# A message-passing layer on one core: gathered rows added by an identity product, laps in pairs, update steps spaced over two laps

## The reference

```python
msg_in = concatenate([nodes[row], nodes[col], edge_features], axis=-1)      # 160 wide
messages = relu(msg_in @ mW1 + mb1) @ mW2 + mb2                             # 128 hidden, 64 out
aggregated = segment_sum(messages, col, num_segments=12500)
upd = relu(concatenate([nodes, aggregated]) @ uW1 + ub1) @ uW2 + ub2
x = layernorm(x + upd)
```

## Time and profile before

| | us |
|---|---|
| median of three runs | 2077.49 |
| lowest and highest of them | 2075.89, 2080.76 |
| the profiled execution | 2080.34 |
| its span, first to last instruction | 2078.6 |

### The profile page before, as it was taken

One profiled execution on the slowest core, in us unless ns is written; L12 is line 12 of the kernel. 1 busy time (PEld: TensorE's weight loads), 2 busy tenths in 40 slices (PEclk: granted clock), 3 DMA queues, 4 the chain that ended last, 5 costly groups with the idle time before them and its releaser, 6 DMA issues. The chain is left out here.

```text
span 2078.6 us, 61063 instructions
## 1 busy us (share of the span) xinstructions
PE 1452.0 (70%) x10272; PEld 1305.0 (63%) x10272; DVE 1428.5 (69%) x7986; ACT 1202.2 (58%) x7120; POOL 1407.3 (68%) x1480
## 2 busy tenths in 40 slices
PE   6866677667666776676667767767767767677765
PEld 5766666566666666666666666666656666566664
DVE  3677677677776777777776667676666676666765
ACT  3366566566565655665656556556556566556563
POOL 1677777777777777777777666666666666666661
PEclk8898888787888888888887778777777777778777
DMA  9833332333333333333322222222222222222221
GB/s 217 231 86 83 82 84 81 80 86 81 82 81 83 85 81 81 85 82 82 79 76 76 69 67 66 69 70 73 66 68 65 70 72 69 68 64 66 72 70 28
DMA packets 179217, 170.23 MB, mean 82 GB/s; under 512 B 78164, under 2 KB 142090, under 8 KB 178842
## 3 DMA queue, kind: packets, MB, share of 16 engines
q0 software_dynamic: 46944, 96.24, 17.8%
q1 hardware_dynamic: 118298, 64.35, 11.4%
q10 hardware_dynamic: 13698, 7.28, 1.7%
HBM read 151.34 MB, written 16.36 MB: 81 GB/s over the span
## 5 line engine op out<-in xcount | busy, mean ns | idle before, releaser
L312 POOL DMA_INDIRECT ag<-src_table,slot_idx x1467 | 1400.7, 955 | 629.4 <-issue 420.2
L290 DVE COPY own_x<-xc 64x4 uint8 x6144 | 682.9, 193 | 131.8 <-issue 124.1
L300 ACT ACTIVATE own_x<-xc 64x4 uint8 x6144 | 634.1, 190 | 183.2 <-issue 182.3
L350 PE MATMUL bank<-picked,picks 128*128 128x128 f32 x3128 | 586.5, 342 | 62.5 <-ACT picks L382 40.0
L350 PEld LDWEIGHTS bank<-picked,picks 128*128 128x128 f32 x3128 | 508.4, 244 | 91.4 <-issue 56.8
L367 PE MATMUL bank<-oh,hid 128*128 128x96 f32 x3128 | 518.2, 321 | 49.8 <-ACT hid L392 49.6
L367 PEld LDWEIGHTS bank<-oh,hid 128*128 128x128 f32 x3128 | 488.2, 238 | 68.6 <-ACT hid L392 59.1
L414 DVE TENSOR_TENSOR hid<-bank,ag 128x512 f32<-128x512 f32 (+1 forms) x391 | 257.4, 658 | 297.2 <-issue 161.1
L382 ACT ACTIVATE picks<-bank 96x512 f32<-96x512 f32 x391 | 230.6, 590 | 225.7 <-PE bank L336 127.3
L392 ACT ACTIVATE hid<-hid 128x512 f32<-128x512 f32 x343 | 215.1, 627 | 241.4 <-DVE hid L414 238.9
L336 PE MATMUL bank<-ident_bf,oh 128*96 128x128 bf16 x1564 | 192.2, 258 | 227.4 <-DVE oh L400 227.2
(11 more groups left out here) (63 smaller groups left out, 446.2 us busy)
## 6 DMA issues: line engine op xcount, KB each, us to landing
picks<-edge_t SPq DMA_DIRECT2D x391, 64.0 KB
ag<-src_table,slot_idx POOLq DMA_INDIRECT x1467
picked<-dst_table SPq DMA_DIRECT2D x391, 48.0 KB
src_table<-ag SPq DMA_DIRECT2D x25, 256.0 KB, 4.1
dst_table<-picks SPq DMA_DIRECT2D x17, 256.0 KB, 4.5
xc<-x_t ACTq DMA_DIRECT2D x8, 400.0 KB, 15.6
resid<-x_rows SPq DMA_DIRECT2D x24, 128.0 KB
out<-resid ACTq DMA_DIRECT2D x24, 128.0 KB
```

The source lines that it names most:

```text
L290: done = copy(own_x[:, c:c + 1].bitcast(u8), xc[0:D, :].bitcast(u8)[:, ds(offset, 4)])
L300: return nc.scalar.activation(to, of, ACT.Copy)
L312: pool.indirect_dma_start(out=ag[:, k, j * DH:(j + 1) * DH], out_offset=None, in_=src_table, in_offset=bass.IndirectOffsetOnAxis(ap=slot_i ...
L350: last = nc.tensor.matmul(ps_h[q][:, j * DH:(j + 1) * DH], picks[:, r, j * P:(j + 1) * P], picked[:, r, :], start=True, stop=j < own)
```

## The change

- `ag[:, k]` is no longer added by VectorE. `hidden` starts with one product of the identity (float32) with the 512 gathered columns (256 for the own group) into `ps_h`, then the own products, then the four products as before, all accumulating. TensorE waits for the gather; `s_pre` is gone, and a gather waits for `s_h` of the group eight before. `relu` reads `ps_h` and writes `hid`.
- VectorE copies 20 own columns a group, ScalarE 12. `own_x` and its list have two buffers: the copies of one whole lap serve the product of the next, which is at k = 4 now. The list comes in one DMA a lap.
- `slot_idx` has two buffers; one DMA a lap, at k=2, brings the next lap's indices.
- Laps are written in pairs in each loop, since the buffers alternate by lap.
- The update of a chunk is spread over two laps, with m1, m2, m3 at k = 3, 5, 7.
- ScalarE does one square root at the very start, ahead of its first copy.

The diff, cut to its core:

```diff
-OWN_K = 5
+OWN_K = 4
...
-OWN_DVE = 16
+OWN_DVE = 20
-OWN_LATE = (UNROLL - OWN_K) * OWN_N
...
-        slot_idx = sb("slot_idx", [P, UNROLL * TPG], i32)
+        slot_idx = sb("slot_idx", [P, 2, UNROLL * TPG], i32)
...
-        own_late = sb("own_late", [1, OWN_LATE], i32)
-        own_early = sb("own_early", [1, OWN - OWN_LATE], i32)
-        own_x = sb("own_x", [D, OWN])
+        own_list = sb("own_list", [1, 2, OWN], i32)
+        own_x = sb("own_x", [D, 2, OWN])
...
+        def fetch_own_list(sp, lap, par):
+
+            sp.dma_start(own_list[0:1, par, :], own_dram[ds(lap + 1, 1), :]).then_inc(s_own_list, 16)
+
+        def load_own(sp, k, lap, par):
+
+            if k == OWN_K + 1 and not (isinstance(lap, int) and lap == ITERS - 1):
                 if not (isinstance(lap, int) and lap == 0):
-                    sp.wait_ge(s_own_dve, (lap - 1) * UNROLL + UNROLL - OWN_K)
-                    sp.wait_ge(s_own_act, (lap - 1) * UNROLL + UNROLL - OWN_K)
-                sp.dma_start(own_late[:, :], own_dram[ds(lap + 1, 1), 0:OWN_LATE]).then_inc(s_own_late, 16)
+                    sp.wait_ge(s_own_dve, lap * UNROLL)
+                    sp.wait_ge(s_own_act, lap * UNROLL)
+                fetch_own_list(sp, lap + 1, 1 - par)
...
+            if k == 0:
+                eng.wait_ge(s_own_list, (lap + 1) * 16)
...
+            if isinstance(lap, int) and lap == ITERS - 1:
+                return
+            at = k * OWN_N
...
-                c = step * OWN_N + a + n
-                done = copy(own_x[:, c:c + 1].bitcast(u8), xc[0:D, :].bitcast(u8)[:, ds(offset, 4)])
+                c = at + a + n
+                done = copy(own_x[:, 1 - par, c:c + 1].bitcast(u8), xc[0:D, :].bitcast(u8)[:, ds(offset, 4)])
...
+        def gather(pool, g, k, lap, par, tiles=TPG):
+
+
+            if k == 0 and not (isinstance(lap, int) and lap == 0):
+                pool.wait_ge(s_idx, lap * 16)
+            wait(pool, s_h, g - UNROLL + 1)
             pool.sem_inc(s_opened, 1)
...
+                    in_offset=bass.IndirectOffsetOnAxis(ap=slot_idx[:, par, c:c + 1], axis=0),
                 ).then_inc(s_gathered[k], 16)
...
+        def hidden(pe, g, k, lap, par):
 
...
-            wait(pe, s_pre, g - 1)
-            own = TPG - OWN_TILES if has_own(k, lap) else TPG
+            wait(pe, s_relu, g - 1)
+            missing = G_END * TPG - T_END if isinstance(g, int) and g == G_END - 1 else 0
+            wait(pe, s_gathered[k], gathered_of(k, lap) - 16 * missing)
+            w = OWN_AT if has_own(k, lap) else TPG * DH
+            nc.tensor.matmul(ps_h[q][:, 0:w], ident[:, :], ag[:, k, 0:w], start=True, stop=False)
+            if has_own(k, lap):
+                pe.wait_ge(s_own_dve, lap * UNROLL)
+                pe.wait_ge(s_own_act, lap * UNROLL)
+                for j in range(OWN_TILES):
+                    at = OWN_AT + j * DH
+                    nc.tensor.matmul(ps_h[q][:, at:at + DH], own_x[:, par, j * P:(j + 1) * P],
+                                     w_src[0:D, :], start=False, stop=False)
             for j in range(TPG):
                 last = nc.tensor.matmul(ps_h[q][:, j * DH:(j + 1) * DH], picks[:, r, j * P:(j + 1) * P],
-                                        picked[:, r, :], start=True, stop=j < own)
-                if j >= own:
-                    if j == own:
-                        pe.wait_ge(s_own_dve, lap * UNROLL)
-                        pe.wait_ge(s_own_act, lap * UNROLL)
-                    last = nc.tensor.matmul(ps_h[q][:, j * DH:(j + 1) * DH],
-                                            own_x[:, (j - own) * P:(j - own + 1) * P],
-                                            w_src[0:D, :], start=False, stop=True)
+                                        picked[:, r, :], start=False, stop=(j == TPG - 1))
             last.then_inc(s_h, 1)
...
+        def relu(g, k):
             act = nc.scalar
             q = k % 2
-            wait(act, s_pre, g + 1)
-            if has_own(k, lap):
-                act.activation(hid[:, q, OWN_AT:], ps_h[q][:, OWN_AT:], ACT.Relu)
-                act.activation(hid[:, q, 0:OWN_AT], hid[:, q, 0:OWN_AT], ACT.Relu).then_inc(s_relu, 1)
-                return
-            act.activation(hid[:, q, :], hid[:, q, :], ACT.Relu).then_inc(s_relu, 1)
+            wait(act, s_h, g + 1)
+            wait(act, s_agg, g - 1)
+            act.activation(hid[:, q, :], ps_h[q][:, :], ACT.Relu).then_inc(s_relu, 1)
...
-        def add_source(g, k, lap):
...
-            dve.tensor_tensor(hid[:, q, 0:w], ps_h[q][:, 0:w], ag[:, k, 0:w], ALU.add).then_inc(s_pre, 1)
...
+        def next_indices(sp, k, lap, par):
+
+            if k != 2 or isinstance(lap, int) and lap == ITERS - 1:
...
-            half, ahead = (0, 1) if k == UNROLL - 1 else (1, 0)
-            for slot in range(half * HALF, (half + 1) * HALF):
-                sp.wait_ge(s_gathered[slot], gathered_of(slot, lap + ahead - 1))
...
+            wait(sp, s_h, lap * UNROLL)
+            w = UNROLL * TPG
+            sp.dma_start(slot_idx[:, 1 - par, :], src_all[:, ds((lap + 1) * w, w)]).then_inc(s_idx, 16)
...
+        def laps(eng, lap, open_update, finish, chunk):
+
+
+            lap(0, 0, None)
+            lap(1, 1, None)
+            with eng.Fori(1, UPD_LAP // 2) as i:
+                lap(i * 2, 0, None)
+                lap(i * 2 + 1, 1, None)
             open_update()
             behind = eng.value_load(path[0:1, 1:2], min_val=0, max_val=NODES)
             with eng.If(behind < 1):
-                with eng.Fori(UPD_LAP, ITERS - 1) as i:
-                    lap(i, i - UPD_LAP)
-                lap(ITERS - 1, CHUNKS - TAIL - 1)
+                for i in range(UPD_LAP, UPD_LAP + 2):
+                    lap(i, i % 2, i - UPD_LAP)
+                with eng.Fori(UPD_LAP // 2 + 1, (ITERS - 1) // 2) as i:
+                    lap(i * 2, 0, i * 2 - UPD_LAP)
+                    lap(i * 2 + 1, 1, i * 2 + 1 - UPD_LAP)
+                lap(ITERS - 1, 0, CHUNKS - TAIL - 1)
+                finish(CHUNKS - TAIL - 1)
                 chunk([CHUNKS - 2, CHUNKS - 1])
...
+                fetch_own_list(sp, 0, 0)
...
+                        next_indices(sp, k, i, par)
+                        load_own(sp, k, i, par)
...
+            act.wait_ge(s_const, 1)
+            act.activation(stat[:, 0, 0:1], eps[:, :], ACT.Sqrt)
...
-                        if c is not None and k == 6:
-                            act_square(c)
                         own_listed(act, k, i)
                         if exists(g + 1):
                             copy_oh(g + 1, (k + 1) % UNROLL)
-                        if c is not None and k == 6:
-                            act_deviation(c)
                         if exists(g):
-                            relu(g, k, i)
-                        own_columns_act(k, i)
-                        if c is not None and k == 3:
+                            relu(g, k)
+                        own_columns_act(k, i, par)
+                        if before(c) and k == 0:
+                            act_square(c - 1)
+                        elif before(c) and k == 2:
+                            act_deviation(c - 1)
+                        elif before(c) and k == 4:
+                            act_store(c - 1)
+                        elif c is not None and k == 5:
                             act_relu(c)
-                        if c is not None and k == 6:
-                            act_store(c)
-                laps(act, lap, open_update, act_chunks)
+
+                def finish(c):
+                    act_square(c)
+                    act_deviation(c)
+                    act_store(c)
+                laps(act, lap, open_update, finish, act_chunks)
...
-                        if exists(g):
-                            add_source(g, k, i)
...
-                        own_columns_dve(k, i)
-                        if c is not None:
-                            if k == 1:
-                                dve_c2(c)
-                            elif k == 2:
-                                dve_stack(c)
-                            elif k == 5:
-                                dve_center(c)
-                            elif k == 6:
-                                dve_variance(c)
-                                dve_normalize(c)
+                        own_columns_dve(k, i, par)
+                        if before(c) and k == 1:
+                            dve_variance(c - 1)
+                        elif before(c) and k == 3:
+                            dve_normalize(c - 1)
+                        if c is not None and k == 1:
+                            dve_c2(c)
+                        elif c is not None and k == 3:
+                            dve_stack(c)
+                        elif c is not None and k == 7:
+                            dve_center(c)
...
+                def finish(c):
+                    dve_variance(c)
+                    dve_normalize(c)
...
```

(24 more changed lines are left out.)

132 lines of the change are left out of this document (51 added, 81 removed).

## The result

The changed kernel takes 1949.53 us (median of four runs, 1947.02 to 1953.16) against 2077.05 (2075.89 to 2080.76): a ratio of 0.9385, 95% interval 0.9365 to 0.9404. The forecast was 1933, with a range of 1914 to 1990. The profiled execution took 1950.72 us for a span of 1949.0 us; the forecast's sum for that span was 1933.8.

The account below looks back on a forecast made before the run. GpSimd bounds the early laps, and the update laps once TensorE's waits go: span 2078.6 - 133.8 (update laps) - 11 (end) = 1933.8 us, or 1933 us as median; range 1914 to 1990.

Parts of the forecast that it names:

- rival A: The forecast itself: GpSimd is the bound from first gather to last, 1917 to 1958 us; chance 0.64.
- The laps: GpSimd's laps of 30 gathers stay at 37.77 us each, with 37.5 and 38.2 as bounds.
- the front: Before the first windows, one list DMA and one ScalarE root more: taken as 0, at most 2 us either way.
- The update laps: GpSimd becomes the bound in the 22 update laps too: 37.77 us for 43.85 each, 133.8 us less.
- rival B: TensorE bounds the update laps if its clock stays as granted: 2021 us, 1987 at a clock of 0.80; chance 0.26.
- The end: From the last gather's start to the span's end: 31.1 us instead of 42.0, 11 less, bounds 3 to 14 less.
- the +3: After the last hidden product: identity product less the add, plus update steps before the last two chunks, +3 us.
- C: The compiler keeps ScalarE's table loads, yet nothing moves: 1933 to 1938 us; lies inside the forecast's own case.
- D: The identity product drops TensorE to its lower clock for good: slower from 0.75 down, some 2370 us at 0.65; chance 0.04.
- E: Another wait takes the place and update laps stay at 42 to 44 us: 2025 to 2069 us; chance 0.06.
- the wait for the square behind the centering: Square of the chunk before, at k=0, waits behind the centering of k=7: a few tenths of waiting.

Follow-up runs that it names:

- experiment 4: The changed kernel with the identity product issued twice for each group: 1942.81 us, ratio 0.9343 to the kernel before.
- experiment 6: The changed kernel with VectorE computing each one-hot once more, into a spare tile: 1985.16 us, ratio 0.9530 to the kernel before.
- experiment 3: The changed kernel with a gather waiting for s_h of the group four before it, not eight: 1965.60 us, ratio 0.9458 to the kernel before.
- experiment 2: The changed kernel without ScalarE's square root at the very start: 1953.36 us, ratio 0.9394 to the kernel before.

## Why the prediction was right, and where it was off

**GpSimd is the bound from the first gather to the last (rival A): right.** It waits for nothing after its first wait, doubling TensorE's addition costs nothing (experiment 4), and lengthening the gathers by 36.7 us moves the last one back by 37.0 (experiment 6). Busy times per lap came as summed: TensorE 29.1 in the first laps (forecast 29.1) and 30.9 in the update laps (32.2), VectorE 29.4 (28.8), ScalarE 20.4 (20.1).

**The laps: a term left out.** Each was put at 37.77 us, as before, with 38.2 as the bound. The first half has 38.01, the update laps 38.43, outside it: together 20.5 us, of which the end, the front and the last lap gave 5.5 back. The last gather starts at 1922.37, not near 1903. "I keep 37.77" took a gather's 0.94 us for a number of GpSimd alone. Experiment 6 shows that it is not: the same gathers take longer when VectorE reads two SBUF inputs just ahead of them. The sum looked at VectorE for its share of time, where the change takes 0.18 us a group away, and not at what its one-hots do to a gather.

**The update laps, 22 x 6.08 = 133.8 us: 119.2 measured.** The mechanism is as put: the waits for indices are gone, and TensorE's waits before m1, m2 and the own products with them. Which part did it? Without the spacing 90 us of 128 stay, without the identity product some 104. The rest (indices in two buffers, the longer lead, the own columns a lap ahead) was never taken away by itself: experiment 3 halves the lead, but with the laps already short. The parts overlap, since each version of the two is short by two or three microseconds a lap and the lead of eight groups lets it be short for thirteen laps or more. The prediction gave the lead no credit of its own.

**The clock (rival B): settled by a run.** It is 0.93 and 0.95 where the forecast asked for 0.85 or more. With the addition on VectorE it is 0.80 and 0.87, with the identity product 0.93 and 0.95, with two 0.99 and 1.00. More work on TensorE gave the higher clock. Single waits still bring the lower level: after 2.00 us idle the product of 1504.07 needs 1.84 us to the next start, the one of 1519.79, after 0.57 us, needs 0.93:

```profile
1504.07 2.05 PE L336 MATMUL bank<-ag,ident 128*128 128x512 f32 x2 [2.00 <-ACT picks L370]
1505.91 1.49 PE L345 MATMUL bank<-picked,picks 128*128 128x128 f32 x6
...
1519.79 1.10 PE L336 MATMUL bank<-ag,ident 128*128 128x512 f32 x2 [0.57 <-DMA ag<-src_table,slot_idx]
1520.72 1.05 PE L345 MATMUL bank<-picked,picks 128*128 128x128 f32 x8
```

The rule of the Trainium skill that stood behind B (TensorE: Matmul & The Clock Gate, "A second HAM failure mode: psum-queue depth-cycling") would, as the prediction read it, have kept the clock near 0.77 for the short idles between groups. They are here, 132.5 us of them before the identity products, and the clock is 0.95: the measurement decides against it for this kernel.

**The end: 31.1 forecast, 26.6 measured.** TensorE was at GpSimd's heels even more closely than put. The last identity product starts 3.1 us after the last gather, where 2.7 + 2 were put, and 23.5 us follow it, for 26.4. So the +3 for the identity product and the steps that move behind k=7 came to about nothing. Whether they cost less than put, or the clock gave it back (0.85 from the last gather on, 0.79 before), isn't separated.

```profile
1922.37 0.94 POOL L297 DMA_INDIRECT ag<-src_table,slot_idx  x1 [0.30 <-issue]
...
1925.42 1.10 PE L336 MATMUL bank<-ag,ident 128*128 128x512 f32 x2 [1.08 <-DMA ag<-src_table,slot_idx]
```

**C, D and E.** C is out: there is one table load. Its price, nothing, wasn't tested, since taking the early root away didn't bring the loads back (experiment 2). D would have needed a clock below 0.75. E: the wait for the square behind the centering, which I had put next, is 0.0 us.

## What to carry to other kernels

Where one engine sets the pace, ask not only how full the others are, but what they share with it: here each one-hot that GpSimd's gather follows closely costs 0.25 us, from a VectorE that is 24% idle. An addition that moves into a product of an engine with time to spare may cost less than nothing: here TensorE's granted clock rose from 0.83 to 0.94 with it. And a deeper lead hides a deficit for only so many laps: see what the last laps and the tail after the last gather do before a version is called free.

## What the runs showed of the hardware

- A gather (128 rows by indices) takes 0.94 us, 1.19 when it starts about 0.2 us behind a VectorE instruction of 128 x 384 with two SBUF inputs, and 1.65 in six cases in which it starts 0.05 us behind a 128 x 256 addition of two SBUF tensors that the 128 x 384 one follows at once. Where two one-hots follow each other (experiment 6), none takes over 1.35.
- Loading a list of offsets from SBUF into an engine's registers takes 62 to 69 ns a column in whole fours from a multiple of four on, and 213 to 235 ns for each other column. With 22 and 26 columns, in halves, two loads of 2.8 us in each group made laps of 69 us, on a chip of the usual kind.
- Doubling a product that TensorE has time for raised its granted clock from 0.94 to 0.99 over the span, and the kernel became no slower.
- On two of four chips the kernel before took 3308 and 3387 us instead of 2079 and 2082. Single instructions of VectorE, ScalarE and GpSimd lasted as long there as elsewhere (a copy 0.19 us in both); the time went into the gaps between them.
